# The front of a two-layer kernel rewritten: bias carried as a feature of x-hat, its transposes kept, tiles grouped by batch, x3 turned by DMA

## The reference

```python
x = L0_attn_x                                   # (2, 2048, 256)
x = x + _layernorm(_L0_attn_ref(_layernorm(x), norm_w, norm_b, qkv_w, qkv_b, proj_w, proj_b))
x = x + _layernorm(_L0_ffn_ref(_layernorm(x), phi, W, b))

# attention without a softmax
h = _layernorm(x, norm_w, norm_b)
q, k, v = split(einsum('btc,oc->bto', h, qkv_w) + qkv_b)
attn = einsum('btc,bsc->bts', q, k) / sqrt(C)
o = einsum('bts,bsc->btc', attn, v)
return residual + einsum('btc,oc->bto', o, proj_w) + proj_b

# feed-forward: 64 experts with 32 slots each
logits = einsum('bmd,dnp->bmnp', x, phi)
dispatch = softmax(logits, axis=0)              # over the two batches
combine = softmax(logits.reshape(b, m, n * p), axis=-1)
slots = einsum('bmd,bmnp->bnpd', x, dispatch)
y = einsum('bnpd,nde->bnpe', slots, W) + b[None, :, None, :]
out = einsum('bnpd,bmnp->bmd', y, combine)
```

## Time and profile before

| | us |
|---|---|
| median of 3 runs (741.16 to 741.33) | 741.33 |
| the profiled execution | 736.78 |
| its span | 734.9 |
| first `slots` of block 0 starts (L1270) | 118.22 |
| first `slots` of block 1 starts | 233.02 |

### The profile page before, as it was taken

One profiled execution on the slowest core, in us unless ns is written; L12 is line 12 of the kernel. 1 busy time (PEld: TensorE's weight loads), 2 busy tenths in 40 slices (PEclk: granted clock), 3 DMA queues, 4 the chain that ended last, 5 costly groups with the idle time before them and its releaser, 6 DMA issues.

```text
span 734.9 us, 12857 instructions
## 1 busy us (share of the span) xinstructions
PE 653.8 (89%) x4086; PEld 394.9 (54%) x4086; DVE 480.4 (65%) x932; ACT 340.1 (46%) x571; POOL 245.2 (33%) x497
## 2 busy tenths in 40 slices
PE   3999668788679999999999997779999999999993
PEld 2765445344234444444444443437777777777773
DVE  4738778887745554645565546777787777777760
ACT  0123366537354333443333332755666555666550
POOL 5521473625130000000000000026665666655666
PEclk9999989999889999999999999989999999999998
DMA  8900001000101343333334446759999999999992
GB/s 292 369 1 1 1 0 44 16 29 36 51 30 58 122 134 125 122 121 121 130 127 129 137 129 223 151 125 208 224 205 226 220 221 218 220 195 235 221 186 60
DMA packets 173471, 100.34 MB, mean 137 GB/s; under 512 B 136065, under 2 KB 161922, under 8 KB 171138
## 3 DMA queue, kind: packets, MB, share of 16 engines
q1 hardware_dynamic: 168944, 82.07, 44.4%
q10 hardware_dynamic: 4498, 17.89, 7.9%
HBM read 43.32 MB, written 23.07 MB: 90 GB/s over the span
## 4 chain that ended last, share of the span: by engine, by line
PE 71%; DVE 13%; issue 4%; POOL 3%; ACT 3%; DMA 3%; SPq 2%; POOLq 0%; DVEq 0%; ACTq 0%
PE psL L1270 22%; PE psL L1372 10%; PE bk L1258 9%; PE bk L1386 6%; PE bk L1390 6%; PE bk L1387 6%; PE bk L1283 4%; PE psL L1129 3%; PE bk L1233 2%; DVE xres L868 2%; DVE r L859 2%; DVE r L857 1%; DMA xres<-in_x 1%; DMA r<-in_ffn_w 1%; DVE xbuf L818 1%
## 5 line engine op out<-in xcount | busy, mean ns | idle before, releaser
L1270 PE MATMUL psL<-r,r_xn 128*128 128x512 f16 x768 | 184.1, 391 | 20.1 <-DVE r L859 19.0
L573 ACT ACTIVATE r<-bk,small 128x512 f32<-128x512 f32 x128 | 81.0, 684 | 151.7 <-PE bk L1258 151.5
L1270 PEld LDWEIGHTS psL<-r,r_xn 128*128 128x128 f16 x768 | 74.3, 100 | 121.8 <-issue 31.8
L1386 PE MATMUL bk<-r_xn,r 128*128 128x256 f16 x512 | 113.9, 273 | 6.9 <-DVE r_xn L1055 4.1
L1387 PE MATMUL bk<-r_xn,r 128*128 128x256 f16 x512 | 113.8, 273 | 0.0
L857 DVE TENSOR_SCALAR r<-r 128x1024 f16<-128x1024 f32 x64 | 47.1, 735 | 72.5 <-ACT r L573 72.4
L1258 PE MATMUL bk<-phs,r_xdT 128*128 128x512 f16 (+1 forms) x384 | 94.0, 382 | 0.0
L1372 PE MATMUL psL<-phs,xT 128*128 128x512 f16 x384 | 88.3, 387 | 5.9 <-DVE small L999 5.1
L465 POOL PARTITION_ALL_REDUCE small<-small x1 | 1.2, 1234 | 251.2 <-DVE small L1070 251.2
L518 ACT ACTIVATE r<-bk 128x512 f32<-128x512 f32 (+2 forms) x113 | 59.8, 531 | 50.2 <-PE bk L1215 33.7
L859 DVE SCALAR_TENSOR_TENSOR r<-r 128x1024 f16<-128x1024 f32 x64 | 81.4, 1272 | 2.2
(11 more groups left out here) (140 smaller groups left out, 885.6 us busy)
## 6 DMA issues: line engine op xcount, KB each, us to landing
r<-in_ffn_w SPq DMA_DIRECT2D x16, 1024.0 KB, 6.5
logit_difference<-r SPq DMA_DIRECT2D x64, 256.0 KB, 2.4
r_xdT<-logit_difference ACTq DMA_DIRECT2D x15, 1024.0 KB, 5.8
xres<-in_x SPq DMA_DIRECT2D x8, 512.0 KB, 10.9
out<-r SPq DMA_DIRECT2D x32, 128.0 KB, 2.2
expert_bias<-r ACTq DMA_DIRECT2D x1, 2048.0 KB, 25.2
r<-in_phi SPq DMA_DIRECT2D x1, 2048.0 KB, 17.6
r<-expert_bias SPq DMA_DIRECT2D x16, 128.0 KB, 6.0
```

Source lines behind the costliest of these rows:

```text
L573: ins = nc.scalar.activation(sF[:, j % 2, s, :], bk[j % 2][:, :], ACT.Sigmoid, scale=kap[:, s:s + 1])
L1270: ins = mm(psL[:, i * 512:(i + 1) * 512], x3n[:, b, j, hx, k * P:(k + 1) * P], shl[:, j % 2, hs, b, :], start=(j == 0 and hx + hs == 0), s ...
L1386: mm(acc, eT[b][:, 0, t, :], yhl[:, b, t, 0, :], start=(t == 0), stop=False)
```

## The change

It rewrites all that runs ahead of block 1. From block 1 on the order is the same.

- **Bias as a feature.** x-hat keeps 255 columns, and column 255 is 1. As the features of a normalized row sum to zero, the missing one is minus the sum of the others: the DVE subtracts its weights from the other columns (`primed_weights`) and puts the bias in its place. S, G, U, R and A are then 256 wide, and `c_row_step` and `abc_step` and all products with one row go, but one: `pb_sel` adds the projection's bias row to A.
- **Transposes kept.** `s_tile` also transposes both halves of the tile (L1193). ACT makes x-hat (`xhat`, L600) in place of the DVE and copies two tiles' transposes to `xx` (`xT_copy`). `h_pair` multiplies two tiles of one batch by A from there (L1234).
- **Known mean of y.** The projection's weights and bias are centred (`bias_columns`, `proj_bias`), so that y has mean zero. ACT sums its squares (`y_squares`, L643) in place of the DVE's bn_stats. The DVE's `add_x` (L945) scales x by r0 and adds h in one instruction, and n0 comes in as the bias of the squares and, later, in `ny`.
- **Groups of one batch.** A group is four tiles of one batch. The orders are `GROUPS_Y` and `GROUPS_X`.
- **x3 turned by DMA.** ACT writes the high half of xd and of x3 (`xd_hi`, `x3_hi`), POOL the low one (`xd_lo`, `x3_lo`), and SP turns both by DMA transpose, 1024 or 2048 columns at once (L314, L317): twelve of them. The stores of d of block 0 move from SP to ACT (`store_d`, L713).
- x of batch 0 is loaded whole ahead of the weights.

```diff
-            load_x(0)
-            load_x(1)
+            for g in range(NG):
+                load_x(g)
...
+            for gi in range(NG):
+                for h in range(2):
+                    j = gi * GJ + 2 * h
+                    sp.wait_ge(xdl_ready, 2 * gi + h + 1)
+                    sp.dma_start_transpose(xx16[:, 1, j:j + 2].rearrange("p j (g t) -> p (j g) t", t=P),
+                                           xdn[:, 2 * h:2 * h + 2].rearrange("p j h c -> p (j h c)")).then_inc(xdT_loaded[2 * gi + h], 16)
+                sp.wait_ge(x3l_ready, 2 * gi + 2)
+                sp.dma_start_transpose(xx16[:, 0, gi * GJ:gi * GJ + GJ].rearrange("p j (g t) -> p (j g) t", t=P),
+                                       x3n[:, 1, gi * GJ:gi * GJ + GJ].rearrange("p j h c -> p (j h c)")).then_inc(xT1_loaded, 16)
...
+        GROUPS_Y = [0, 1, 4, 5, 2, 6, 3, 7]
+        GROUPS_X = [0, 4, 1, 5, 2, 6, 3, 7]
...
+            def y_squares(i, tt):
...
+                for t in tt:
+                    act.wait_ge(y_added, GJ * i + t + 1)
+                    if GJ * i + t >= 4:
+                        act.wait_ge(ssq_ready, GJ * i + t - 3)
+                    nc.scalar.activation(xbuf[:, t, :], xy[:, b, j + t, :], ACT.Square, bias=n0[:, b, j + t:j + t + 1],
+                                         accum_out=ssq[:, b, j + t:j + t + 1]).then_inc(ssq_ready, 1)
...
+            def store_d(j):
+
+                act.wait_ge(d_copied, j + 3)
+                act.dma_start(d_dram[j, :, 0:512], dS[:, j % 2, :]).then_inc(d_stored[j % 2], 16)
...
+            for j in range(NJ):
+                dispatch(0, j)
+                if j == 0:
+                    y_squares(5, four)
+                    x3_float(3)
+                if j == 1:
+                    xd_hi(1)
+                    x3_hi(3)
+                if j == 2:
+                    y_squares(6, four)
+                    x3_float(4)
+                    x3_hi(4)
...
+                store_d(j)
...
+            def add_x(i):
...
+                    V.scalar_tensor_tensor(xy[:, b, j + t, :], xres[:, b, j + t, :], r0[:, b, j + t:j + t + 1],
+                                           h_bank(s)[:, t % 2], ALU.mult, ALU.add).then_inc(y_added, 1)
...
+                for k in range(K):
+                    o = t % 2 * C + k * P
+                    ins = nc.tensor.transpose(bk[2 + p % 2][:, o:o + P], xbuf[:, t % 4, k * P:(k + 1) * P], ident[:, :])
                 ins.then_inc(xh_used, 1)
...
+            pe.wait_ge(phi_split, 1)
+            pe.wait_ge(y_added, 16)
+            d_first(0)
+            d_first(1)
+            pe.wait_ge(y_added, 24)
+            for j in range(NJ):
+                if j % GJ == 0:
+                    pe.wait_ge(x3l_ready, 2 * (j // GJ + 1))
+                slots(0, j)
+                if j + 2 < NJ:
+                    d_first(j + 2)
                 else:
...
+                    d_tile(1, j + 2 - NJ)
+                if j in (2, 3):
+                    h_pair(12 + j)
```

More of the change, by code:

```diff
@@ new lines, in _ @@
+            xd_lo(0, 1)
+            y_terms(3)
+            x3_lo(1)
+            x3_terms(2)
+            x3_terms(3)
+            y_terms(4)
+            xd_diff(1, 0)
+            xd_diff(1, 1)
+            xd_lo(1, 0)
+            xd_lo(1, 1)
+            x3_lo(2)
+            y_terms(5)
+            x3_lo(3)
+            x3_terms(4)
+            y_terms(6)
+            x3_terms(5)
+            x3_lo(4)
+            xd_diff(2, 0)
+            xd_diff(2, 1)
+            xd_lo(2, 0)
+            xd_lo(2, 1)
@@ L464, in _ @@
+            y_terms(7)
+            x3_lo(5)
+            x3_terms(6)
+            x3_lo(6)
+            x3_terms(7)
+            xd_diff(3, 0)
+            xd_diff(3, 1)
+            xd_lo(3, 0)
+            xd_lo(3, 1)
+            x3_lo(7)
+            pool.wait_ge(ry_ready, XG)
+            own.add(nc.gpsimd.tensor_tensor(ny.rearrange("p (b j) -> p b j", b=B), n0, ry, ALU.mult))
             pool.wait_ge(gmax_in, 2)
@@ new lines, in x3_float, with x3_hi @@
+            def x3_float(i):
+                b, j = tiles(GROUPS_X[i])
+                act.wait_ge(r3_ready, i + 1)
+                for h in range(2):
+                    for t in (j + 2 * h, j + 2 * h + 1):
+                        ins = nc.scalar.activation(xy[:, b, t, :], xres[:, b, t, :], ACT.Identity,
+                                                   bias=n3[:, b, t:t + 1], scale=r3[:, b, t:t + 1])
+                    ins.then_inc(x3_ready, 1)
+            def x3_hi(i):
+                b, j = tiles(GROUPS_X[i])
+                act.wait_ge(x3_ready, 2 * i + 2)
+                copy(x3n[:, b, j:j + GJ, 0, :], xy[:, b, j:j + GJ, :]).then_inc(x3h_ready, 1)
@@ new lines, in store_d @@
+            def store_d(j):
+                act.wait_ge(d_copied, j + 3)
+                act.dma_start(d_dram[j, :, 0:512], dS[:, j % 2, :]).then_inc(d_stored[j % 2], 16)
+            four = range(GJ)
+            y_squares(1, four)
+            y_squares(2, four)
+            x3_float(0)
+            x3_hi(0)
+            x3_float(1)
+            y_squares(3, four)
+            xd_hi(0)
+            x3_hi(1)
+            y_squares(4, four)
+            x3_float(2)
+            x3_hi(2)
+            act.wait_ge(phi_split, 1)
@@ L1237, in x3_transpose @@
[L1237 to L1252 removed]
+            h_pair(3)
@@ L1254, in d_tile @@
+            pe.wait_ge(xT_evac, NJ)
+            for s in range(4, 14):
+                h_pair(s)
             def d_tile(nb, j):
```

864 lines of the change are left out of this document (347 added, 517 removed).

## The result

The changed kernel takes **690.62 us** (median of 4 runs, 690.46 to 691.38), 0.932 of the time before (95% interval 0.930 to 0.934); forecast were 692.4, from 681 to 708. The profiled execution takes 690.47 us, its span 688.7. The kernel before does not always end at the same place: its runs beside the experiments lie between 735.6 and 742.3, and the profiled one (736.78) is near the lower end.

What follows compares the result with a forecast made beforehand. Ahead of block 1 the kernel was taken as bound by waits in a ring of engines. Gains of 8.4 + 18.4 + 22.1 = 48.9 us off the median 741.33 gave 692.4 us, range 681 to 708.

Steps and rivals of the forecast that it cites:

- a ring of waits: Ahead of block 1: no engine is full; each works in written order and waits for small pieces from the others.
- ACT waiting for POOL's small terms: Block 0: a sign that would show the prediction right; no size given for the sign itself.
- Stage A: Start to the end of the last S tile: 56.5 us before, 48.1 forecast, 8.4 less.
- the wait for the primed weights: S tiles: PE at tile 14 at 23.9, weights ready at 24.6, so PE waits 0.7 us.
- the split of phi is done after the last of the S tiles, beside them until about 44: S tiles: the split keeps the DVE until about 44 us; now it is done after the last of them.
- Stage B: Last S tile to the first slots: 61.7 us before, 43.3 forecast, 18.4 less.
- the square: ACT's squares of y: 0.55 us each taken, bounds 0.40 and 0.75.
- the turn of 1024 columns: DMA transposes on SP: 3.5 us taken, bounds 2.2 and 7.9; no cost up to 8.
- Stage C: Block 0, first to last slots: 113.4 us before, 91.3 forecast, 22.1 less.
- 20.0 of ACT's own work and 13 of waits: First round of block 0: 33 us, from ACT's 20.0 plus 13 of waits for POOL's terms.
- looser-ring rival: DVE and POOL meet less often than laid out; block 0 ends 9 us sooner, 683 us; chance 0.15.
- The rival in which turns decide: Twelve turns in one SP queue set block 0; 12.9 us each cancels its gain, 16 makes 777; chance 0.02.

Runs made afterwards that it cites:

- e11_lo_twice: The changed kernel with POOL's low half of x3 made twice in each of the eight groups; 705.46 us.
- e4_bn_stats: The changed kernel with the squares of y taken off ACT and the variance of y made by bn_stats on the DVE again; 690.87 us.
- e5_store_on_sp: The changed kernel with the sixteen stores of d of block 0 back on SP, between the DMA turns; 691.65 us.
- e9_two_terms: The changed kernel with POOL's terms of the sixth group of y and fifth of x3 moved ahead of two low halves of x3; 687.34 us.
- e6_order_dve_pool: The changed kernel with the same instructions in another order on POOL and the DVE alone; 676.63 us.
- c0_again: The changed kernel run once more, unaltered, as a yardstick; 690.47 us.
- e1_load: The changed kernel with parameters loaded behind two groups of x again instead of four, and the work on them moved to match; 690.39 us.
- e7_order_all: The changed kernel with ACT and PE reordered too, POOL and the DVE much as in e6_order_dve_pool; 674.89 us.
- e2_load_phi: As e1_load, with POOL's reduction of phi's maximum also moved ahead of the residual terms of batch 1; 690.31 us.

## Why the prediction was right, and where it was off

**What bounds the kernel: a ring of waits.** Right, and shown: added work on the one place of the ring that is short (e11_lo_twice) costs 14.8 us of 19.0, and work taken from elsewhere (16 us of ACT in e4_bn_stats, sixteen stores in e5_store_on_sp) gives nothing, though the squares went to the DVE. The most direct evidence is the order alone: two calls of POOL moved give 3.3 us (e9_two_terms), a new order of POOL and the DVE 14.0 (e6_order_dve_pool). Right was also ACT waiting for POOL's small terms, with 30.6 us the second largest wait.

**Stage A: gain 5.1 in place of 8.4.** The tiles cost what was forecast (0.87 us each). The term that was mis-sized is the wait for the primed weights: 2.60 us and not 0.7 (0.53 in c0_again), and behind it the first four products ran at about half clock (granted 0.54 from 26.1 to 29.8, against 1.00 in c0_again), 3.68 in place of 1.89. The parameters were ready at 15.6 (15.3 forecast). But behind them the sum left out the reduction and scaling of the projection's weights (0.67 + 0.17), and POOL's product took 3.68 and not 2.9. Half again as many columns had been priced at a third more; at half more it is 3.2, and in e1_load, with no bias sum beside it, it took 3.44. Of the DVE's bias sums beside it one took 3.66 us (a sum alone is 0.41):

```profile
15.61 3.68 POOL L430 TENSOR_TENSOR r_xn<-r_xn 128x1536 f32<-128x1536 f32 x1 [1.28 <-DMA r_xn<-in_proj_wT]
```

```profile
15.91 3.66 DVE L871 CUSTOM_DVE_ANT_0 r<-r_xn 128x256 f32<-128x256 f32 x1
```

The stage ended 3.3 us later than forecast. Of that about 1.0 passed on to block 1, by ACT's copy of R, which stood 1.04 us (c0_again), and the rest was hidden: `add_x` could not start before 54.25 anyway. The step "the split of phi is done after the last of the S tiles, beside them until about 44" is the one that failed. It ended at 54.3, because POOL's reduction of the maximum came at 46.16, behind 5.55 us in which POOL waited for nothing that the profile shows. Without them, an estimate from the same rows, it would have ended at 48.8 and gated nothing, but not at 44 either: POOL's own queue kept the reduction until 40.6, and the maximum had been ready since 35.5. With that gate Stages A and B are one stage of 95.7 us against 91.4 forecast.

**Stage B: gain 17.4 of 18.4.** Two terms were missing and two were too high. Missing: the split of phi (1.1 ahead of `add_x`, whose h pair was done at 53.2) and the table that ACT loads ahead of its first sigmoid:

```profile
90.92 1.28 ACT L700 ACT_TABLE_LOAD   x1
```

The trace of the kernel before has the same load in the same stage, so this term could have been in the sum:

```profile
111.34 1.28 ACT L573 ACT_TABLE_LOAD   x1 [1.25 <-issue]
```

The Trainium skill (ScalarE: Activation LUTs, What ACT_TABLE_LOAD costs) gives 1.283 us for the load, and the trace agrees. It adds a drain of 1.38 us, 2.66 together; the changed kernel's trace shows none, for ACT's copy ends at 90.90 and the first sigmoid starts at 92.21, and the measurement decides.

The residual of the fourth group also stood beside POOL's work, 3.52 in place of 1.67, but it is not on the chain that ended last: there ACT's `x3_float` at 87.74 waits for the terms of the third group, which stand in POOL's queue behind its low halves.

```profile
83.55 3.52 DVE L962 SCALAR_TENSOR_TENSOR xres<-r_y,small,xres 128x256 f32<-128x256 f32 x4 [5.62 <-POOL small L395]
```

Too high: the square, for which no row existed. The upper row had also been scaled wrongly: 1.24 us with half of it fixed is 0.78 for 256 columns and not 0.6. The square takes 0.49 us from one to the next, and its read of the accumulator lies beside the next one:

```profile
64.44 0.49 ACT L643 ACTIVATE xbuf<-r_y,small 128x256 f32<-128x256 f32 x1
64.84 0.18 ACT L643 ACTIVATION_READ_ACCUMULATOR xbuf<-r_y,small 128x1 f32 x1
64.93 0.49 ACT L643 ACTIVATE xbuf<-r_y,small 128x256 f32<-128x256 f32 x1
```

By the Trainium skill (ScalarE: Activation LUTs, What ACT_TABLE_LOAD costs) an estimate of 0.50 had stood beside the 0.55 taken, and the trace agrees with it.

The other was the turn of 1024 columns, whose landings (L314) were under the 3.5 taken:

```profile
DMA to landing us min/median/max: 3.1/3.2/4.8
```

The two missing terms make 2.4 us, the fourteen squares on the path give back 0.8, and the turn was off the path. The stage was 1.0 over its forecast, so the other terms together were 0.6 too high.

**Stage C: gain 23.6 in place of 22.1.** The rounds were 30.1, 25.2, 20.1, 14.4 against 33, 22, 22, 14: the sum is right, the shares are not. The reading "20.0 of ACT's own work and 13 of waits" for the first round was too simple. The stores (2.1 in that round) cost nothing on the path (e5_store_on_sp), and taking the squares off ACT, at 13.4 us more for the DVE, gained nothing (e4_bn_stats): ACT's work mostly fills the time until POOL's terms come. So the size of the round came from POOL's queue, and the 13 us of waits were the true half of the sum.

**The bounds between DVE and POOL.** The looser-ring rival did not come: both wait for each other in single rows. In Stage C a `residual` of four takes 3.53 and 4.49 us where 1.67 is usual, and POOL's power 1.99 where 1.01 is. `add_x`, which reads one operand from PSUM, kept its 0.4 beside POOL's work, as I had taken it:

```profile
102.92 1.62 DVE L945 SCALAR_TENSOR_TENSOR r_y<-xres,small,bk 128x256 f32<-128x256 f32 x4
```

```profile
100.10 3.31 POOL L487 TENSOR_TENSOR r<-r 128x512 f16<-128x512 f32 x2 [0.63 <-ACT r L587]
103.37 2.13 POOL L471 TENSOR_TENSOR r_xn<-r_y,r_xn 128x1024 f16<-128x1024 f32 x1
```

By the experiments the strict form, in which either always waits for the other's end, is too hard (17.7 for 14.8, 5 for 0), and the form without any gave too little in two runs (10 for 14.0, 13.3 for 14.8). For e7_order_all both promised too much (24 and 19 for 15.7). That the truth lies between is an argument from the layout; no run isolates it.

**The rival in which turns decide.** It had its point at 12.9 us a turn. With 3.2 it is far off, and even twice 3.2 costs 1.8 us in all.

**From the stages to the time.** Forecast were 48.9 us off the median. The profiled executions have 46.3, and the medians 50.7, since the runs of the kernel before that stand beside it (741.16 to 741.33) end 4 us above its profiled one. That the median fell within 1.8 us of the forecast is in part luck: the stages gained 2.6 us less than forecast, and where the runs of the kernel before happened to end made that good.

## What to carry to other kernels

Where no engine is full, find the queue in which a small result that others wait for stands behind large work that nobody waits for yet; the view of waits names the pair, the chain shows what stood in between, and moving two calls is worth more than moving 16 us of work between engines. Before pricing an added instruction, ask whether its engine waits at that place: here work in front of a wait was free, and work in the queue that the others wait for cost 14.8 us of 19.0. A gate that hides a delay on one engine (`add_x` at 54.25) need not hide it on another: follow each engine's own queue across it. When an order is tuned up to some point of the program, look at what feeds the first step behind that point.

## What was not expected of the hardware

- POOL stood 5.6 us ahead of the PARTITION_ALL_REDUCE for phi, and, where ordinary work followed at once (e2_load_phi), 6.7 us behind it, with nothing to wait for. In the changed kernel POOL has nothing to do for 12.1 us behind it, so that a gap there would not show.
- One instruction of the DVE can take 3.66 us in place of 0.41 when a large one of POOL has just begun: it ended at 19.57, POOL's at 19.29.
- Of the same program, two executions differed by 2.1 us in PE's wait for the primed weights, and the four products behind it took 1.99 us in one (granted clock 1.00) and 3.68 in the other (0.54), and still ended within 0.6 us of each other.
